# One ring of row sets for all expert jobs, zeroed from its own strip, with row copies that wait tile by tile

## The reference

```python
x = x + _L0_attn_ref(_layernorm(x), ...)   # A: linear attention, a recurrence over the 1024 rows
x = x + _L0_ffn_ref(_layernorm(x), ...)    # B: 8 experts of width 352, the 2 best of each row
x = x + _L1_attn_ref(_layernorm(x), ...)   # C: convolution, then a recurrence with 16 states per column
x = x + _L1_ffn_ref(_layernorm(x), ...)    # D: 8 experts of width 128, the 2 best, and 2 shared ones
```

```python
scores = jax.nn.softmax(logits, axis=-1)
w, idx = jax.lax.top_k(scores, TOPK)
h = silu(xt @ W1[e].T) * (xt @ W3[e].T);  out = h @ W2[e].T
y = sum over the two experts of  w * out
```

## Time and profile before

| | before |
|---|---|
| device time, median of 3 | 1800.45 us |
| span of the profiled execution | 1833.6 us |
| DVE busy in it | 1361.4 us (74%) |
| PE busy in it | 1401.7 us (76%) |
| ACT busy in it | 981.4 us (54%) |
| POOL busy in it | 929.9 us (51%) |
| sent by the SP queue (q1) | 277672 packets, 336.05 MB |

### The profile page before, as it was taken

One profiled execution on the slowest core, in us unless ns is written; L12 is line 12 of the kernel. 1 busy time (PEld: TensorE's weight loads), 2 busy tenths in 40 slices (PEclk: granted clock), 3 DMA queues, 4 the chain that ended last, 5 costly groups with the idle time before them and its releaser, 6 DMA issues.

```text
span 1833.6 us, 29178 instructions
## 1 busy us (share of the span) xinstructions
PE 1401.7 (76%) x9192; PEld 943.1 (51%) x9192; DVE 1361.4 (74%) x2543; ACT 981.4 (54%) x1663; POOL 929.9 (51%) x571
## 2 busy tenths in 40 slices
PE   6674899988999789688578567787836776767668
PEld 3342577755776556555355434565613553435345
DVE  6793969788997889649586588288759579639836
ACT  2213262638756666378264554677446575477332
POOL 1000422385451856828838588400278737852875
PEclk9886899999999999989889579889969788879879
DMA  9995373757884669858477678888468767876952
GB/s 238 162 184 116 90 208 119 212 137 249 281 263 137 215 218 292 230 145 281 148 213 169 185 231 220 231 291 281 125 200 247 200 202 250 225 209 210 287 111 50
DMA packets 320067, 369.53 MB, mean 202 GB/s; under 512 B 33801, under 2 KB 260521, under 8 KB 319657
## 3 DMA queue, kind: packets, MB, share of 16 engines
q1 hardware_dynamic: 277672, 336.05, 62.8%
q0 software_dynamic: 42240, 31.61, 9.6%
HBM read 306.09 MB, written 63.42 MB: 202 GB/s over the span
## 4 chain that ended last, share of the span: by engine, by line
PE 23%; issue 16%; POOL 16%; DVE 15%; ACT 11%; SPq 9%; DMA 7%; another core or an unknown queue 1%; POOLq 0%; DVEq 0%; ACTq 0%
POOL x L886 7%; POOL rows_D L867 5%; PE bank L991 3%; DVE arena_c L1516 3%; POOL rows_B L867 2%; PE bank L1063 2%; SPq L664 2%; SPq L686 2%; DVE arena_c L1502 2%; DMA x<-outs,slot_idx 2%; DMA arena_c<-bc_rows 2%; DVE arena_c L1511 2%; PE bank L1098 2%; DVE arena_a L1443 1%; PE bank L951 1%
## 5 line engine op out<-in xcount | busy, mean ns | idle before, releaser
L886 POOL DMA_INDIRECT x<-outs,slot_idx x240 | 465.4, 1939 | 205.2 <-issue 110.7
L991 PE MATMUL bank<-arena_c,ident 128*128 128x512 f32 x512 | 289.2, 702 | 96.9 <-DVE arena_c L1502 95.9
L1516 DVE TENSOR_TENSOR_SCAN arena_c<-arena_c 128x1024 f32<-128x1024 f32 x128 | 292.1, 2283 | 1.8
L909 PE MATMUL bank<-xT_ring,mix 128*128 128x128 f16 (+1 forms) x1296 | 240.9, 225 | 58.0 <-DVE mix L1688 16.7
L910 PE MATMUL bank<-xT_ring,mix 128*128 128x128 f16 (+1 forms) x1296 | 240.4, 225 | 0.0
L911 PE MATMUL bank<-xT_ring,mix 128*128 128x128 f16 (+1 forms) x1296 | 240.3, 225 | 0.0
L1063 PE MATMUL bank<-mix 128*128 128x128 f32 (+1 forms) x1296 | 192.2, 295 | 60.4 <-ACT yrow L1319 36.2
L1063 PEld LDWEIGHTS bank<-mix 128*128 128x128 f32 (+1 forms) x1296 | 172.9, 205 | 96.0 <-issue 86.0
L991 PEld LDWEIGHTS bank<-arena_c,ident 128*128 128x128 f32 x512 | 104.9, 222 | 218.9 <-DVE arena_c L1502 121.7
L867 POOL DMA_INDIRECT rows_D<-xrow,slot_idx x112 | 187.7, 1676 | 40.1 <-issue 30.1
L867 POOL DMA_INDIRECT rows_B<-xrow,slot_idx x128 | 182.2, 1423 | 46.0 <-issue 35.0
(11 more groups left out here) (225 smaller groups left out, 2460.4 us busy)
## 6 DMA issues: line engine op xcount, KB each, us to landing
arena_c<-bc_rows SPq DMA_DIRECT2D x256, 512.0 KB
mix<-weights_B SPq DMA_DIRECT2D x168, 352.0 KB
mix<-weights_B SPq DMA_DIRECT2D x168, 192.0 KB
outs<-yrow SPq DMA_DIRECT2D x156, 128.0 KB
mix<-weights_D SPq DMA_DIRECT2D x144, 128.0 KB
xg<-rows_B SPq DMA_DIRECT2D x84, 129.0 KB
xg<-rows_D SPq DMA_DIRECT2D x72, 129.0 KB
mix<-weights_D SPq DMA_DIRECT2D x144, 64.0 KB
```

The costliest lines, as they stand in the source:

```text
L886: pool.indirect_dma_start(out=x[:, b, j, :], out_offset=None, in_=y_d[q], in_offset=bass.IndirectOffsetOnAxis(ap=slot_idx[:, q % RJ, c, i ...
L909: pe.matmul(o, hi, xh, start=True, stop=False)
L991: last = pe.matmul(bank[C_BANKS[h]][:], ident[:], half(hb[:, n % RR, :], h), start=(n == 0), stop=(n == NS - 1))
L1516: dve.tensor_tensor_scan(hb[:, n % RR, :], dA[:, n % RDA, :], hb[:, n % RR, :], 0.0, ALU.mult, ALU.add).then_inc(c_scan.sem, 1)
```

## The change

There are three sets of rows instead of six, and job q uses set q modulo 3, whichever layer it belongs to. Before it scatters, a job from number 3 on waits for the gathers of job q - 3 (before: of the third job before it of the same layer).

The zeros have a place of their own: the last 430 words of the third slot of `h_ring`. A set is written in packets of 430 words, 1720 bytes, 12 for each of 128 partitions, 1536 in all. The first `m_norm` has no wait for zeros any more. The first use of that slot of `h_ring` on DVE has it (`hidden_slot`). SP issues the zeroing of sets 1 and 2 where it issued that of the sets of layer B, and no zeroing stands ahead of `keep`.

The semaphore of the second scatters is split into four, one for each group of four tiles. `m_hi` waits for the group that it will overwrite, `load_rows` and the first scatter of a job for all groups.

```diff
-    ROW_SETS = {"B": 3, "D": 3}
+    ROW_SETS = 3
...
-        xs_d = {(s, i): dram(f"rows_{s}{i}", [SLOTS, D + 1], F32) for s in "BD" for i in range(ROW_SETS[s])}
+        xs_d = [dram(f"rows_{i}", [SLOTS, D + 1], F32) for i in range(ROW_SETS)]
...
-        zero_rows = xn[:, :, :].rearrange("p j d -> p (j d)")[:, 0:D + 1]
...
+        SLOT_WORDS = SLOTS // P * (D + 1)
+        ZERO_WORDS = max(n for n in range(1, 513) if SLOT_WORDS % n == 0)
+        zeros = mix2[:, W_WORDS + (RS + RH) * U_WORDS - ZERO_WORDS:W_WORDS + (RS + RH) * U_WORDS]
...
-        def all_scattered(w, q):
-            if q >= 0:
-                w.wait_ge(scattered, 16 * sum(JT[:q + 1]))
+        def all_scattered(w, q, groups=range(MT // TH)):
+            for g in groups:
+                if any(n > g * TH for n in JT[:q + 1]):
+                    w.wait_ge(scattered_second[g], 16 * TH * sum(n > g * TH for n in JT[:q + 1]))
...
-            def zero(s, i):
-                sp.dma_start(xs_d[s, i].rearrange("(n p) f -> p n f", p=P),
-                             zero_rows.unsqueeze(1).broadcast_to([P, SLOTS // P, D + 1])).then_inc(s_zeroed[s, i], 16)
-
-            zero("B", 0)
+            def zero(i):
+                sp.dma_start(xs_d[i].rearrange("(p r) f -> p (r f)", p=P).rearrange("p (n w) -> p n w", w=ZERO_WORDS),
+                             zeros.unsqueeze(1).broadcast_to([P, SLOT_WORDS // ZERO_WORDS, ZERO_WORDS])).then_inc(s_zeroed[i], 16)
+
+            zero(0)
...
-            for i in range(1, ROW_SETS["B"]):
-                zero("B", i)
+            for i in range(1, ROW_SETS):
+                zero(i)
...
-            for i in range(ROW_SETS["D"]):
-                zero("D", i)
...
-                    for r in range(q):
-                        if JOBS[r][0] == s and NTH[r] == NTH[q] - ROW_SETS[s]:
-                            job_gathered(wt, r)
+                    if q >= ROW_SETS:
+                        job_gathered(wt, q - ROW_SETS)
...
-                        oob_is_err=True).then_inc(scattered if c else scattered_first[j], 16)
+                        oob_is_err=True).then_inc(scattered_second[j // TH] if c else scattered_first[j], 16)
...
-                else:
-                    for key in xs_d:
-                        wt.wait_ge(s_zeroed[key], 16)
-                    wt.wait_ge(s_kept["B"], 16 * (4 + NC["B"] + 1))
                 normalise(s, b, xn, m_normed.sem, range(h * TH, (h + 1) * TH))
...
-                all_scattered(wt, q - 1)
+                all_scattered(wt, q - 1, (i * NH + h,))
...
             def hidden_slot(n):
+                if n == RH - 1:
+                    for i in range(ROW_SETS):
+                        wt.wait_ge(s_zeroed[i], 16)
+                    wt.wait_ge(s_kept["B"], 16 * (4 + NC["B"] + 1))
```

More of the change, by code:

```diff
@@ L160, in build @@
     SLOTS = MOST_BLOCKS * NB
-    ROW_SETS = {"B": 3, "D": 3}
-    NTH = [sum(j[0] == s for j in JOBS[:q]) for q, (s, _) in enumerate(JOBS)]
+    ROW_SETS = 3
+    FIRST_OF = [next(q for q, j in enumerate(JOBS) if j[0] == s) for s, _ in JOBS]
     PARTS_UP_TO = [[sum(len(j[1]) > i for j in JOBS[:q + 1]) for i in range(MOST)] for q in range(len(JOBS))]
@@ L349, in build @@
             kept_at += cols_kept
+        assert kept_at <= W_WORDS + (RS + RH) * U_WORDS - ZERO_WORDS and ZERO_WORDS <= U_WORDS
         g_lg, g_sel = (sb(f"g_{n}", [P, MT, E]) for n in ("lg", "sel"))
@@ L432, in build @@
             "P": [("ready", "B")] + [st for q in range(len(JOBS)) for st in
-                                     [("ready", "D")] * (JOBS[q][0] == "D" and NTH[q] == 0) + prepare(q)],
+                                     [("ready", "D")] * (JOBS[q][0] == "D" and FIRST_OF[q] == q) + prepare(q)],
             "X": [st for q in range(len(JOBS)) for st in scatters(q)],
@@ L586, in build @@
         s_kept = {s: sem(f"weights_kept_{s}") for s in "BD"}
-        s_zeroed = {key: sem(f"rows_zeroed_{key[0]}{key[1]}") for key in xs_d}
+        s_zeroed = [sem(f"rows_zeroed_{i}") for i in range(ROW_SETS)]
         x_in = [sem(f"x_loaded_{b}") for b in range(B)]
@@ L615, in build @@
         scattered_first = [sem(f"rows_scattered_first_{j}") for j in range(MT)]
-        scattered = sem("rows_scattered")
+        scattered_second = [sem(f"rows_scattered_second_{g}") for g in range(MT // TH)]
         gathered_first = [sem(f"outs_gathered_first_{j}") for j in range(TT)]
@@ L682, in _ @@
             sp.dma_start(Wd["B"][:, rows:P, W13["B"] + c * D:W13["B"] + (c + 1) * D].rearrange("e p d -> p e d"),
-                         zero_rows[rows:P, 0:D].unsqueeze(1).broadcast_to([P - rows, E, D])).then_inc(s_kept["B"], 16)
-            def zero(s, i):
-                sp.dma_start(xs_d[s, i].rearrange("(n p) f -> p n f", p=P),
-                             zero_rows.unsqueeze(1).broadcast_to([P, SLOTS // P, D + 1])).then_inc(s_zeroed[s, i], 16)
-            zero("B", 0)
+                         zeros[rows:P, 0:D].unsqueeze(1).broadcast_to([P - rows, E, D])).then_inc(s_kept["B"], 16)
+            def zero(i):
+                sp.dma_start(xs_d[i].rearrange("(p r) f -> p (r f)", p=P).rearrange("p (n w) -> p n w", w=ZERO_WORDS),
+                             zeros.unsqueeze(1).broadcast_to([P, SLOT_WORDS // ZERO_WORDS, ZERO_WORDS])).then_inc(s_zeroed[i], 16)
+            zero(0)
             load_x(2)
@@ L799, in _ @@
             pool.memset(neg_half[:], -0.5).then_inc(s_cons0, 1)
-            pool.memset(zero_rows, 0.0).then_inc(s_cons0, 1)
+            pool.memset(zeros, 0.0).then_inc(s_cons0, 1)
             wt.wait_ge(s_cons0, 3)
@@ L867, in m_scatter @@
                     pool.indirect_dma_start(
-                        out=xs_d[s, NTH[q] % ROW_SETS[s]], out_offset=bass.IndirectOffsetOnAxis(ap=slot_idx[:, q % RJ, c, j:j + 1], axis=0),
+                        out=xs_d[q % ROW_SETS], out_offset=bass.IndirectOffsetOnAxis(ap=slot_idx[:, q % RJ, c, j:j + 1], axis=0),
                         in_=xrow[:, j, :], in_offset=None, bounds_check=SLOTS - 1,
-                        oob_is_err=True).then_inc(scattered if c else scattered_first[j], 16)
+                        oob_is_err=True).then_inc(scattered_second[j // TH] if c else scattered_first[j], 16)
             def m_gather(q, i, c, first):
```

4 lines of the change are left out of this document (2 added, 2 removed).

## The result

The changed kernel takes 1776.66 us (median of 5 executions, 1775.56 to 1787.37) beside 1805.9 us (5 executions, 1800.25 to 1806.42) for the kernel before: a ratio of 0.985, 95% interval 0.982 to 0.988. The prediction starts from 1800.45 us, the median of the first three executions; its 1775.5 us is a ratio of 0.986. The spans of the changed kernel's three profiled executions are 1785.5, 1771.4 and 1774.7 us.

What follows compares the result with a forecast made beforehand. No engine was busy over 76% of the span, so waits were taken to bound it; 22.0 + 5.0 + 1.3 - 2.9 = 25.4 us off 1833.6 gives 1808.2, scaled by 0.982 to 1775.5 us; range 1757 to 1795 us.

Steps and rivals of the forecast that it cites:

- The start: First m_norm no longer waits for zeros and kept weights, so m_lo comes at 138.9 instead of 160.9: 22.0 us gained.
- The rival that gave half of the pause to the profile: Start: the profile's excess may sit there; with half of it 11.9 us are gained, 1789 us; chance 0.17.
- DVE is late next: Start: m_lo could start at 138.5 us, but DVE is free only at 138.8, so DVE sets its time.
- The long packets: Start, ahead of layer C's weights: zeros in 1720-byte packets go faster, 5 us gained, between 0 and 6.26.
- The ring: Jobs 4 to 8: half the sets add waits for gathers of job q - 3, already passed by POOL; costs 0.
- Job 5: ACT's m_hi goes on 16 us earlier, but slower scatters delay SP's rows and C row: 2.9 us lost.
- I take 3.6 us: Job 5: assumed price of one POOL scatter beside busy DVE, between the 3.2 and 3.9 us seen.
- The formula: Job 5: 17.3 us of DVE work pass 4.8 of 12 scatters, the other 7.2 take 9.6 us, ending at 930.7.
- The sign of "scatters of 3 us and more before it": Near job 5 in the profile after: scatters of 3 us and more before DVE's pause for a B or C row.
- Job 4: DVE's 5.82 us pause goes, while two scatters and SP come 4.5 us later: 1.3 us gained.
- Was hidden: 0: The remaining m_hi wait, besides those at jobs 4 and 5, was hidden, so removing it gains 0.
- the slower rival: Jobs 3 and 4: scatters beside busy DVE starve the SP queue; over 0.5% slower from 4.5 us each; chance 0.05.

Runs made afterwards that it cites:

- second profile of before: The unchanged kernel before, run and profiled once more: 1805.46 us beside 1804.01, ratio 1.000, span 1802.8 us.
- e6: The changed kernel with zeros written in packets of 516 bytes instead of 1720: 1791.7 us, ratio 0.992 to the kernel before.
- e11: The kernel before with zeros from the hidden ring's strip and 1720-byte packets, still six sets and no tile groups: 1784.43 us, ratio 0.990.
- e9: A separate small kernel timing only row scatters on POOL, alone and beside DVE work or loads: 0.97 us alone, 1.97 beside DVE products, once 41.25.
- e1: The changed kernel without tile groups, so row copies wait for all scatters of the job before: 1785.13 us, ratio 0.989 to the kernel before.

## Why the prediction was right, point by point

The places and the waits at the start are the prediction's. That the total fits is in part luck, as its terms for the tile groups are wrong in size, one of them in sign.

**The start: right in place, the size taken too large from one profile.** The 22.0 us were DVE's pause. It is gone, for the reason given; but in the second profile of before it was 12.46 us, so a good 9 us of the step belonged to the one profiled execution. The rival that gave half of the pause to the profile named the right weakness. Together with the C weights' wait (6.68 there) that makes 19.1 us, and the first placement came 20.7 us earlier (173.15 to 152.5, the mean of three). "DVE is late next" was right: `m_lo` has no wait. `keep` had more cover than said: it was issued by 98 us, where its landing had been put at 113. The price of a set, 14.9 us at 177 GB/s, was read well: e6 has 176 in its stretch of zeros.

**The long packets: 5 us predicted, the whole 6.3 to 6.7 us of the wait removed.** 3.2 to 6.3 us of this reach the first placement. 252 GB/s, the row that I took as nearest, was under the 287 measured with nearly nothing but zeros.

**The ring: 0, right.** No wait for gathers of job q - 3 shows up. That the ring itself brings the start nothing once the zeros have their strip and long packets (e11) the prediction didn't say; it gave three sets fewer 45 us of backlog, which was true and without worth.

**Job 5: the mechanism right, the price and the count wrong.** As predicted ACT's wait fell under 9 us (6.19), and in its place DVE waits for a C row behind `load_rows`, 7.18 us where 940.0 - 921.1 = 18.9 were predicted. Two steps failed. One is "I take 3.6 us". DVE works from 871.27 to 888.67 us, 17.4 us as predicted, and in this time POOL gets eight scatters and a copy of the gate column done, one scatter every 2.1 us:

```profile
866.79 0.97 POOL L868 DMA_INDIRECT rows<-xrow,slot_idx  x1 [0.30 <-issue]
...
871.89 0.97 POOL L868 DMA_INDIRECT rows<-xrow,slot_idx  x1 [0.30 <-issue]
...
885.92 2.94 POOL L868 DMA_INDIRECT rows<-xrow,slot_idx  x1 [0.31 <-issue]
```

The window around it shows that DVE wasn't busy all the time before that, for 22.41 of 28 us: it paused for 4.50 us ahead of 871.27, and from 866.79 on four scatters ran in this pause at 0.97.

```profile
861.00:889.00 28.00, 20.02 (x128) 13.72 (x125) 22.41 (x23) 15.84 (x21) 23.12 (x16) 0.88 0.30 104
```

The other is the count. The formula puts 12 scatters behind 903.8 us, but two of the 12 had started by then, the second of them at 903.04:

```profile
903.04 0.97 POOL L867 DMA_INDIRECT rows_D<-xrow,slot_idx  x1 [0.30 <-issue]
```

With 2.2 us, the price of e9 beside a full DVE, and 10 scatters, 17.3 us let 7.9 through, and 2.1 remain at 1.34: 903.8 + 17.3 + 2.8 = 923.9 instead of 930.7, which is 3.9 us gained instead of 2.9 lost. Measured: 4.6 us gained in the mean, 4.0 without the first profile of before. The sign of "scatters of 3 us and more before it" didn't come: of the last twelve the longest took 2.94.

**Job 4: wrong sign.** Predicted 1.3 us gained, measured 6.3 lost. The delay of SP was predicted well, 4.5 us, and measured as 4.8 (the rows are loaded 81.4 us after the placement of job 3 instead of 76.6). The step that failed keeps a gain beside it, since DVE's 5.82 us were to go. The two scatters took 4.79 and 2.54 us, and DVE's pause didn't go: it waits for PE and ACT, who wait for the rows of job 3, which the same scatters hold up.

**The remaining waits of `m_hi`: one right, two left out.** "Was hidden: 0" was said of a wait of 4.50 us at job 1, and is right: the stage from the first placement to the second takes 75.7 us in the mean with and without groups. But the first profile has no such wait behind that of job 5, and the second profile of before has one of 7.80 us at job 6 and one of 4.58 us at job 7. By the pooled means groups took 4.2, 2.8 and 5.6 us from the stages behind job 5, more than the two terms that were worked out; the last of the three has no such wait behind it.

**The sum.** Predicted were 27.0 us at the start and -1.6 by the groups, scaled from the high span. Measured were 20.7 at the start (against the second profile). For the groups it is some 10 us by the pooled means, 4.0 from the placement of job 3 on against the second profile of before, and nothing against e1. The total of the profiles is 1802.8 - 1777.2 (the mean of three) = 25.6 us; the medians of the three comparisons differ by 29, 33 and 15 us. So the forecast came out where it did partly because an overstated start and an understated second part cancel. The chain that the slower rival needs, scatters at 3.8 us and more, didn't occur: the 2.1 us above stay far under it.

**What stays open.** Why single scatters in the full kernel took 5 to 6 us beside DVE (5.86 at 857.59 us in the changed kernel), when e9 has 1.97 or 41.25: neither the phase of DVE's steps nor the part of other instructions was varied. With it stays open where the 3.2 and 3.9 us of rows 10 come from. And what the groups are worth, between nothing and 10 us.

## What to carry to other kernels

Where a source buffer of background DMAs delays its next use, try the two cheap cures first and apart, another place for the source and longer packets; either a shorter backlog or a free buffer may be enough, and a ring built on top may bring nothing. A wait that is split into finer ones can starve whoever lived on the pause: before it is removed, list what runs in the pause (here POOL's last scatters) and who needs that next. And a pause read from one profile is one sample, in either direction: in the profile whose span lies 30 us over that of the second, the pause at the start was 22.06 us and became 12.46, but DVE's pause at job 4 was 5.82 and became 10.92. A second profile of the same kernel is the cheapest correction.

## What was not expected of the hardware

A row scatter of 128 x 516 bytes costs POOL 0.97 us, the same at a DMA share of 0.15 and of 1.02, and 1.97 us beside DVE products with both inputs in SBUF. Once it was held for 41.25 us, until the last of a row of 48 products. With zeros in packets of 1720 instead of 516 bytes the queues moved 287 instead of 176 GB/s.
